# The opening of a fused transformer kernel: first loads, first products and the second tile's contexts in another order

## What is computed

```python
def _L0_xattn_ref(latents, context, ...):
    lat = layernorm(latents, ln_l_w, ln_l_b)
    ctx = layernorm(context, ln_c_w, ln_c_b)
    q = (lat @ Wq)   # 16 heads of 64
    k, v = jnp.split(ctx @ Wkv, 2, axis=-1)
    attn = softmax(clip(einsum('bhnd,bhsd->bhns', q, k) * D ** -0.5, -11, 11))
    return einsum('bhns,bhsd->bhnd', attn, v) @ Wo + bo
...
x = x + _L0_xattn_ref(_layernorm(x), ctx_1024, ...)   # latents are normalised twice
```

## Time and profile before

| | |
|---|---|
| median of 3 runs | 1004.1 us (1000.98 to 1010.59) |
| the profiled execution | 1003.49 us, its span 1001.8 us |
| TensorE busy | 949.6 us, 95% of the span |
| VectorE, ScalarE, GpSimd busy | 613.0, 446.1, 169.3 us |
| mean granted clock of TensorE | 0.981 |

### The profile page before, as it was taken

How to read it: one execution, slowest core, us unless ns; L and a number is a source line. 1 busy time by engine, 2 the same in 40 slices (tenths; PEclk the granted TensorE clock), 3 DMA queues, 4 the chain that set the end, 5 groups by cost and what they waited for, 6 DMA issues and landing times.

```text
span 1001.8 us, 25859 instructions
## 1 busy us (share of the span) xinstructions
PE 949.6 (95%) x10657; PEld 815.0 (81%) x10657; DVE 613.0 (61%) x1448; ACT 446.1 (45%) x892; POOL 169.3 (17%) x357
## 2 busy tenths in 40 slices
PE   5899999999999989999879999997999999999998
PEld 5788888888888777887669999995888888877887
DVE  5655754654532655667798787776787763554242
ACT  3333332433332476654236666652435343673241
POOL 2312112113112213334320000013113000101000
PEclk9999999999999999999979999997999999999999
DMA  9443142131210292000049999952312002000000
GB/s 321 129 106 74 33 106 68 39 85 42 45 37 7 67 381 98 3 12 24 20 129 332 380 357 358 328 129 57 59 36 45 3 2 76 2 2 1 8 14 22
DMA packets 158611, 101.14 MB, mean 101 GB/s; under 512 B 102104, under 2 KB 148128, under 8 KB 157984
## 3 DMA queue, kind: packets, MB, share of 16 engines
q1 hardware_dynamic: 156960, 95.31, 32.0%
q0 software_dynamic: 1536, 4.20, 1.3%
HBM read 82.96 MB, written 16.52 MB: 99 GB/s over the span
## 4 chain that ended last, share of the span: by engine, by line
PE 82%; DVE 9%; ACT 5%; issue 2%; DMA 1%; POOL 0%; SPq 0%; DVEq 0%; ACTq 0%; POOLq 0%
PE ps L642 9%; PE ps L657 8%; PE ps L2367 8%; PE ps L2380 6%; PE ps L2703 6%; PE ps L674 3%; PE ps L1486 3%; PE ps L1195 3%; PE ps L1583 3%; PE ps L596 2%; PE ps L693 2%; PE ps L626 2%; PE ps L1525 2%; PE ps L1120 2%; PE ps L1130 2%
## 5 line engine op out<-in xcount | busy, mean ns | idle before, releaser
L2367 PE MATMUL ps<-moe_xT,ew 128*128 128x128 f32 x736 | 91.3, 278 | 2.2 <-issue 1.2
L2367 PEld LDWEIGHTS ps<-moe_xT,ew 128*128 128x128 f32 x736 | 87.6, 195 | 3.2 <-DVE moe_xT L2453 1.9
L785 ACT ACTIVATE x0pT<-ps 128x512 f32<-128x512 f32 x64 | 38.2, 598 | 111.1 <-PE ps L657 111.1
L1029 POOL TENSOR_SCALAR x0pT<-x0pT 128x512 f32<-128x512 f32 x64 | 40.6, 635 | 188.3 <-ACT x0pT L785 187.2
L2703 PE MATMUL ps<-f,ffw 128*128 128x512 f32 x256 | 60.7, 398 | 0.8 <-issue 0.6
L2703 PEld LDWEIGHTS ps<-f,ffw 128*128 128x128 f32 x256 | 48.9, 192 | 12.0 <-issue 0.9
L642 PE MATMUL ps<-x0wv_hi,x0cT_hi 128*128 128x512 f32 x128 | 53.6, 418 | 4.2 <-DVE x0A_lo L915 4.2
L2380 PE MATMUL ps<-ew_2hi,eh_hi 128*128 128x256 f32 x184 | 55.4, 301 | 1.7 <-DVE eh_lo L2506 1.3
L2316 DVE TENSOR_TENSOR ew_2lo<-ew,ew_2hi 128x1024 fp32r<-128x1024 f32 x46 | 55.9, 1216 | 0.0
L2563 POOL DMA_INDIRECT yg<-moe_out,slot x16 | 16.3, 1017 | 230.9 <-DMA moe_out<-moe_y 163.5
L915 DVE TENSOR_TENSOR x0A_lo<-ps,x0A_hi 128x512 fp32r<-128x512 f32 x64 | 39.8, 683 | 23.4 <-ACT x0A_hi L776 23.3
(11 more groups left out here) (336 smaller groups left out, 2416.6 us busy)
## 6 DMA issues: line engine op xcount, KB each, us to landing
ew<-L_ffn_W_dram SPq DMA_DIRECT2D x46, 1024.0 KB, 7.9
x0cin<-ctx_dram SPq DMA_DIRECT2D x8, 512.0 KB, 4.7
x1cin<-ctx_dram SPq DMA_DIRECT2D x64, 64.0 KB, 2.3
x0cn_rows<-x0cn SPq DMA_DIRECT2D x7, 512.0 KB, 2.8
x0cn_blocks<-x0cn_rows SPq DMA_DIRECT2D x56, 64.0 KB, 2.4
x0att_rows<-x0att SPq DMA_DIRECT2D x14, 256.0 KB, 2.5
x0att_blocks<-x0att_rows SPq DMA_DIRECT2D x56, 64.0 KB, 2.7
moe_out<-moe_y SPq DMA_DIRECT2D x23, 128.0 KB, 4.4
```

The lines of the kernel that those rows point to most:

```text
L785: nc.scalar.activation(g.pT[:, u, :], ps[:, S_BANK[u % 2], :], ACT.Exp, scale=64.0 ** -0.5).then_inc(C0.exp, 1)
L1029: nc.gpsimd.tensor_scalar(g.pT[:, u, :], g.pT[:, u, :], high, low, ALU.min, ALU.max).then_inc(C0.clip, 1)
L2367: last = nc.tensor.matmul(ps[:, n % 3, j * BT:j * BT + BT], ew1[b % NW][:, i, f * P:f * P + P], xT[b % 2][:, i, :], start=(i == 0), stop=( ...
```

## The change

Loads: of the constants only the identity (64 of 297 KB) is loaded at first, the rest behind contexts 1. Opening: TensorE makes 18 products on zeros (pT, set by VectorE) before it waits for any load, then turns key weights, latents and contexts in this order; VectorE normalises the latents ahead of the contexts (norm_first), ScalarE copies K(0) to K(2) and VectorE K(3). Tile 0: turn_context(1), cT(1) and cT_split(1) stand on VectorE and ScalarE behind the work of tile 0, no longer in its middle. SyncE: the 15 loads of later weights are issued behind turn_rows(1).

```diff
-        FILLS = [(("x0", 0), k) for k in ("cT0", "cT1", "K0", "K1", "lat", "K2", "K3", "q0", "q1", "A00", "A01", "A10", "A11", "v0", "v1", "A20", "A21", "A30", "A31")]
+        FILLS = [(("x0", 0), k) for k in ("K0", "K1", "K2", "K3", "lat", "cT0", "cT1", "q0", "q1", "A00", "A01", "A10", "A11", "v0", "v1", "A20", "A21", "A30", "A31")]
...
+            pe.wait_ge(C0.zeros_lat_ones, 1)
+            for _ in range(18):
+                nc.tensor.matmul(ps[:, S_BANK[0], 0:P], g.pT[:, 0, 0:P], g.pT[:, 0, 0:P], start=True, stop=True, skip_group_check=True)
+            pe.wait_ge(ld["const"], 32)
+            for i in range(4):
+                fill_K(i)
+            fill_lat(0)
             fill_cT(0, 0)
             fill_cT(0, 1)
-            fill_K(0)
-            fill_K(1)
-            fill_lat(0)
-            fill_K(2)
-            fill_K(3)
             fill_q(0, 0)
...
+            K(0)
+            K(1)
+            K(2)
+            lat(0)
             cT(0)
-            K(0)
-            lat(0)
-            K(2)
             act.wait_ge(ld["x0v"], 16)
...
                 exp(t, 3)
+                if nxt and t > 0:
+                    cT(t + 1)
                 if nxt:
-                    cT(t + 1)
                     lat(t + 1)
...
+                if t == 0:
+                    cT(1)
...
+            def norm_first():
+                dve.wait_ge(ln_rstd, 1)
+                nc.vector.tensor_scalar(g.lat[:, :], x[:, 0, :], ln_mv[:, 4, 0:1], ln_rs[:, 4:5], ALU.subtract, ALU.mult).then_inc(C0.zeros_lat_ones, 1)
+                dve.sem_inc(dve_go, 1)
+                dve.wait_ge(C0.zeros_lat_ones, 2)
+                nc.vector.bn_stats(g.ln_st[:, 4, :], g.lat[:, :]).then_inc(ln_stats, 1)
+                dve.wait_ge(ln_stats, 2)
+                dve.sem_inc(dve_go, 1)
+                nc.vector.bn_aggr(ln_mv[:, 4, :], g.ln_st[:, 4, :]).then_inc(ln_aggr, 1)
+                for k in range(4):
+                    last = nc.vector.tensor_scalar(g.cn[:, k, :], g.cin[:, 0, k, :], ln_mv[:, k, 0:1], ln_rs[:, k:k + 1], ALU.subtract, ALU.mult)
+                last.then_inc(ln_done, 1)
+                dve.wait_ge(ln_rstd, 2)
+                nc.vector.tensor_scalar(g.lat[:, :], g.lat[:, :], ln_mv[:, 4, 0:1], ln_rs[:, 4:5], ALU.subtract, ALU.mult).then_inc(ln_done, 1)
+
+            nc.vector.memset(g.pT[:, 0, 0:P], 0.0).then_inc(C0.zeros_lat_ones, 1)
             dve.sem_inc(rn_rstd, 2)
             norm(0, 0)
             dve.wait_ge(ld["x"], 16)
             norm(0, 1)
-            norm(0, 2)
+            norm_first()
             dve.wait_ge(ld["const"], 32)
-            norm(0, 3)
+            K(3)
             cT(0)
-            K(1)
-            K(3)
             cT_split(0)
...
-            dve.wait_ge(ld["rest"], 32)
+            dve.wait_ge(ld["rest"], 48)
             for t in range(T):
                 nxt, more = t + 1 < T, t + 2 < T
                 if more:
                     norm(t + 2, 0)
-                if nxt:
+                if nxt and t > 0:
                     turn_context(t + 1)
                 if t > 0:
                     turn_att(t - 1, 0)
                     turn_att(t - 1, 1)
                     v(t, 3)
-                if nxt:
+                if nxt and t > 0:
                     cT(t + 1)
                     cT_split(t + 1)
...
+                    turn_context(1)
+                    cT(1)
                 attend(t, 0)
+                if t == 0:
+                    cT_split(1)
...
-                ln_rstd_pool(pool, 1, 2 * t + 1)
+                ln_rstd_pool(pool, 1, 2 * t + 1, 4 if t == 0 else 0)
...
-            whole(cst[:, :], a["consts"], ld["const"])
+            whole(ident, a["consts"][:, C_IDENT:C_IDENT + P], ld["const"])
             whole(col[:, :], a["cols"], ld["const"])
             whole(X0.wk[:, :, :], weight("L0_xattn_Wkv")[:, :, 0:INNER], ld["x0k"])
             whole(X0.wq[:, :, :], weight("L0_xattn_Wq"), ld["x0q"])
             whole(X0.wv[:, :, :], weight("L0_xattn_Wkv")[:, :, INNER:], ld["x0v"])
             ctx_tile(1, 1)
+            whole(cst[:, P:C_ALL], a["consts"][:, P:C_ALL], ld["rest"])
             whole(X0.wo[:, :, :], weight("L0_xattn_Wo"), ld["x0o"])
             whole(x[:, 2:T, :], x_in[:, 2:T, :], ld["rest"])
...
-            for i, w in enumerate(("wq", "wkv")):
-                whole(w_mla[:, :, 64 * i:64 * i + 64], weight("L0_attn_" + w), ld["mla"])
-            for i, w in enumerate(("wqr", "wqr_swapped", "wkr", "wkr_swapped")):
-                whole(w_mla[:, :, P + P * i:2 * P + P * i], weight("L0_attn_" + w), ld["mla"])
-            whole(w_mlao[:, :, :], weight("L0_attn_wo"), ld["mla"])
-            sp.wait_ge(pool_setup, 4)
-            whole(w_mlac[0:64, 0:P], a["L0_attn_wqc"], ld["mla"])
-            whole(w_mlac[64:P, P:2 * P], a["L0_attn_wkc"], ld["mla"])
-            whole(w_mlac[64:P, 2 * P:2 * P + D], a["L0_attn_wv"], ld["mla"])
-            whole(wg[:, :, 0:E], weight("L0_ffn_Wg"), ld["wg"])
-            for i, w in enumerate(("Wq", "Wk", "Wv", "Wo")):
-                whole(w_sq[0][:, :, i, :], weight("L0_ffn_" + w), ld["sq0"])
             def turn_rows(t):
                 sp.wait_ge(ln_done, 2 * t + 1)
+                if t > 1:
+                    sp.wait_ge(C0.cn_in, 128 * (t - 1))
...
                     turn_rows(t)
+                if t == 1:
+                    for i, w in enumerate(("wq", "wkv")):
+                        whole(w_mla[:, :, 64 * i:64 * i + 64], weight("L0_attn_" + w), ld["mla"])
+                    for i, w in enumerate(("wqr", "wqr_swapped", "wkr", "wkr_swapped")):
+                        whole(w_mla[:, :, P + P * i:2 * P + P * i], weight("L0_attn_" + w), ld["mla"])
+                    whole(w_mlao[:, :, :], weight("L0_attn_wo"), ld["mla"])
+                    sp.wait_ge(pool_setup, 4)
+                    whole(w_mlac[0:64, 0:P], a["L0_attn_wqc"], ld["mla"])
+                    whole(w_mlac[64:P, P:2 * P], a["L0_attn_wkc"], ld["mla"])
+                    whole(w_mlac[64:P, 2 * P:2 * P + D], a["L0_attn_wv"], ld["mla"])
+                    whole(wg[:, :, 0:E], weight("L0_ffn_Wg"), ld["wg"])
+                    for i, w in enumerate(("Wq", "Wk", "Wv", "Wo")):
+                        whole(w_sq[0][:, :, i, :], weight("L0_ffn_" + w), ld["sq0"])
                 if t + 2 < T:
                     sp.wait_ge(ln_done, 2 * t + 2)
                     ctx_tile(t + 2, t % 2)
```

More of the change, by code:

```diff
@@ L321, in ln_statistics, with ln_rstd_pool @@
             last.then_inc(ln_aggr, 1)
-        def ln_rstd_pool(pool, k, idx):
+        def ln_rstd_pool(pool, k, idx, first=0):
+            c = slice(first, first + k)
             pool.wait_ge(ln_aggr, idx + 1)
-            nc.gpsimd.tensor_tensor(ln_ve[:, 0:k], ln_mv[:, 0:k, 1], eps[:, 0:k], ALU.add).then_inc(ln_eps, 1)
+            nc.gpsimd.tensor_tensor(ln_ve[:, c], ln_mv[:, c, 1], eps[:, c], ALU.add).then_inc(ln_eps, 1)
             pool.wait_ge(ln_eps, idx + 1)
-            nc.gpsimd.tensor_tensor(ln_rs[:, 0:k], ln_ve[:, 0:k], neghalf[:, 0:k], ALU.pow).then_inc(ln_rstd, 1)
+            nc.gpsimd.tensor_tensor(ln_rs[:, c], ln_ve[:, c], neghalf[:, c], ALU.pow).then_inc(ln_rstd, 1)
         def ln_apply(dve, srcs, dsts, idx):
@@ L488, in build @@
             cT_lo = sem("c0_cT_lo")
-            ones = sem("c0_ones")
+            zeros_lat_ones = sem("c0_zeros_lat_ones")
             scores = sem("c0_scores")
@@ L546, in build @@
         _more += [(("x1", t), k) for t in range(T) for k in ("q", "k1")]
-        RS = Ring([ps[:, i, :] for i in range(4)], FILLS, ("cT1", "q1", "K1", "K3", "v1", "v3", "v5", "v7", "T1", "rope", "k", "pv", "y", "y2", "router", "rank"),
+        RS = Ring([ps[:, i, :] for i in range(4)], FILLS, ("cT1", "q1", "K3", "v1", "v3", "v5", "v7", "T1", "rope", "k", "pv", "y", "y2", "router", "rank"),
                   SA.fill, SA.by_act, SA.by_dve, _more)
@@ L667, in values @@
                     if t == 0:
-                        pe.wait_ge(C0.ones, 1)
+                        pe.wait_ge(C0.zeros_lat_ones, 3)
                 for par in range(2):
@@ L976, in dve_x0 @@
             A_lower(0, 1)
-            nc.vector.memset(g.v[:, :, :, 64:VW], 1.0).then_inc(C0.ones, 1)
+            nc.vector.memset(g.v[:, :, :, 64:VW], 1.0).then_inc(C0.zeros_lat_ones, 1)
             v(0, 1)
@@ L2962, in _ @@
         def _(pe):
-            pe.wait_ge(ld["const"], 32)
             x0 = pe_x0(pe)
```

## The result

| | before | after |
|---|---|---|
| median | 1002.67 us (20 runs, 999.61 to 1012.33) | 1009.65 us (20 runs, 1005.75 to 1016.18) |
| the profiled execution and its span | 1003.49, 1001.8 us | 1009.19, 1007.5 us |
| TensorE busy | 949.6 us | 957.9 us |
| mean granted clock, profiled execution | 0.981 | 0.976 |

The ratio is 1.0064, with a 95% interval of 1.0043 to 1.0085: the change costs 6 to 7 us. The forecast was 1002.0 with a range to 1008. TensorE is busy 8.3 us longer: 7.1 us are the products on zeros, in a time that was idle, and y(0) alone takes 2.9 us more for the same products.

A forecast was written before the change was run, and what follows sets the result against it. It took TensorE, holding 82% of the span, as the bound. Start -1.7, tile 0 -4.3, new idle before y(0) +2.8 and clock after it +1.7 sum to -1.5 us: from 1003.49 to 1002.0 us, range 996 to 1008.

The forecast's parts named there:

- The bound: Whole kernel: TensorE holds 82% of the span; gains lie only in its idle or slow time in the first stage.
- The start: First 23 us: first value product earlier by 0.8 us with slow transposes, 2.5 with fast ones; 1.7 us taken.
- Tile 0: Middle of tile 0: 2.57 us of idle and 1.7 us of low clock go, together 4.3 us gained.
- rival 4: Tile 0: VectorE's work piles up and v(1,0) waits, giving back up to 2 us, 1004; chance 0.05.
- The place where the gain would stop: At y(0), behind SyncE's chain of issues and landings: it can move forward only by 2.2 us less the rows' delay.
- turn_rows(2) at 49.4: SyncE's queue: behind 15 weight loads taking 8.7 us, this issue comes at 49.4 instead of 51.63, 2.2 us earlier.
- the part on the queue: SyncE's queue before y(0): weights in flight delay the rows 0 to 1.5 us, 0.7 taken; idle becomes 3.0 us.
- The clock after it: Behind the new idle before y(0): lower granted clock costs 1.7 us, as after the 2.57 us gap in tile 0.
- my sum: Whole kernel: start -1.7, tile 0 -4.3, new idle before y(0) +2.8, clock after it +1.7, together -1.5 us.
- The slower one: SyncE's queue: 15 issues take over about 10 us, y(0) idles 6.2 us, clock falls; +2.8, 1006.3; chance 0.12.
- Rival 1: SyncE's queue is quick: y(0) waits 2 us or less, clock stays; -4.5, 999, or -6.8, 996.7; chance 0.28.
- Rival 3: Opening: warm-up has no effect, all 26 transposes take 0.215 us, start gains only 0.8; -0.6, 1002.9; chance 0.13.

The follow-up runs named there:

- e8: The changed kernel once more, unchanged, measured beside e5 and e6; 1008.09 us, ratio 1.0036 to the kernel before.
- e4: The kernel before with only the turn of contexts 1 moved behind the rest of tile 0; 1000.27 us, ratio 0.9965.
- e10: The changed kernel with the eleven small loads back in the opening, only the four w_sq loads behind turn_rows(1); 997.85 us, ratio 0.9916.
- e2: The kernel before with only the 15 loads of later weights moved behind turn_rows(1); 1004.91 us, ratio 0.9996.
- e1: The changed kernel with the 15 loads back behind the load of contexts 2, ahead of turn_rows(1); 997.03 us, ratio 0.9928.
- e9: The changed kernel with the four w_sq loads back in the opening, only the eleven small loads behind turn_rows(1); 1001.92 us, ratio 0.9960.
- e6: The changed kernel with 28 unused products that TensorE makes while it waits for y(0); 1004.96 us, ratio 1.0007 to the kernel before.
- e3: e1 without the 18 products on zeros; 999.33 us, ratio 0.9959 to the kernel before.
- e5: The changed kernel with the 15 loads issued behind both halves of the attention rows of tile 0; 998.95 us, ratio 0.9941.
- e12: e1 with all 297 KB of constants in one first load ahead of the key weights; 1000.96 us, ratio 0.9937 to the kernel before.
- e11: e1 with 28 products on zeros instead of 18; 996.74 us, ratio 0.9912 to the kernel before.

## Why the prediction was wrong

**What held.** The bound, and that there are only two places to gain. The start: forecast 1.7 with ends of 0.8 and 2.5, measured 2.65 in after and 0.25 in e8, the same kernel, by how early the keys land (9.71 and 11.20) and whether they run fast. Both lie outside those ends, so this term held only in its sign. Tile 0: forecast 4.3, measured 4.4, with a clock of 1.00 from 47 to 51, and e4, which has nothing else, puts y(0) 4.5 us earlier beyond its earlier v(0,0). No new wait at v(1,0): I had 57.5 with the turned contexts ready at 53.3, both before the gain of the start, and it is 54.83 and 50.5, so rival 4 did not occur. The place where the gain would stop: y(0), behind a chain of issues and landings. And turn_rows(2) at 49.4 less the start's 1.7, that is 47.7: measured 47.47. Some luck is in that: against the measured start it is 0.7 later than booked, since the block issues of tile 1 took 5.16 us instead of 4.04 and the 15 loads 8.1 instead of 8.7.

**The step that failed** is in the part on the queue: "less what the 2 MB of weights still in flight delay the rows; at 329 GB/s the last megabyte takes 3.1 us and was begun some 3 us earlier, so between 0 and 1.5; I take 0.7". The rows landed 7.2 us after issue instead of 2.8, 4.4 later, and the idle before y(0) was 7.40 us instead of the 3.0 forecast. Two things were wrong in this term. The rate was that of the opening; from 47 to 51 the queues moved 237 GB/s at a DMA share of 0.97. And I left out contexts 3, 512 KB, which stand directly in front of the rows. The four w_sq loads and the contexts are 1.57 MB; at 237 GB/s they take 6.6 us, and the first was issued at 44.84, 2.6 us before the rows: 4.0 us, close to the 4.4 measured. The window of that rate was picked after the result, so the sum is a check and no proof of how the queues share. In other runs it comes out less well or better: e10 and e8 have the same 4.0 and landed 4.7 and 4.8 late, e2 has 1.6 and landed 1.4 late, e1 has 0.3 and landed 0.7 late. The blocks took 5.13 us of issue instead of 4.04, 1.1 more (4.04 again in e8, so this varies), and the attention rows went over their part of the chain 1.2 us faster (60.38 to 70.70, against 59.09 to 70.64), so the end of it came at 75.49.

**The clock after it** was the second mis-sized term, 1.7 booked and 2.9 measured: y(0) took 6.62 us instead of 3.69. I took the loss of the gap of 2.57 us; after a gap of 7.4 the clock is 0.50 until 82 us, nearly all of y(0). e9 is the other side of it: 2.10 us of idle there, and y(0) ran in 3.69. With the wait filled by products (e6) the median is some 3 us lower.

With the measured sizes my sum runs: -2.65 -4.4 +7.2 of additional idle +2.9 = +3.05, and the trace of after has 3.06 at 82.92 and at 118.21. The mechanism was the forecast one, its two prices were too small, and with them the sign came out wrong: y(0)'s start is set by the chain of SyncE (76.17 before, 76.31 after), so the gain of tile 0 is given back there in full, and the idle time then charges the clock on top. The gain of the opening is another thing, since that chain starts with it: turn_rows(1) goes out at 30.73 in after and at 33.13 in e8, v(0,0) starts at 20.02 and 22.42, y(0) at 76.31 and 78.67, with the same idle in front (7.40, 7.36). So in after the chain is 2.8 us longer from the start on than before, and the 2.65 of the opening just hide it.

**The rivals.** The slower one came nearest, +2.8 forecast. Its condition, that the 15 issues take longer than about 10 us, was not met: they took 8.1 us. It was the landing that made its case. I gave it 0.12, since I saw bytes in flight as a small correction to the count of issues. Rival 1 is what e1 shows for the kernel with the loads elsewhere: "with the full 2.5 of the start and no wait at all, -6.8", measured -6.6. Rival 3 is refuted as a rule: after makes 16 key transposes in 1.94 us, and e3, without the zeros, in 3.65. But in four of the ten executions with zeros the keys took 2.93 to 3.52 us, so it describes part of what happens. The rule of the Trainium skill, "TensorE: Matmul & The Clock Gate", Part 4 (PE-mode transpose), that the full clock does not engage for transpose mode, does not agree with these rows.

**The rest of the median.** 3.06 us at y(0) are not the 6.4 of the ratio. I had written that a time over 1008 would mean that something after 80 us moved; only a part of the miss is of that kind. Two things vary between executions. One is the opening: e8 has the late keys and is 4.95 us behind after y(0), for 4.7 of the median. The other is the granted clock further on: after's profiled execution has the two stretches near 362 and 838 us, e8's has not, and such stretches are found in other traces too (0.91 from 780 to 800 us in before, 0.83 from 820 to 840 in e5 and in e12). The mean clock recorded with each execution tells of it: over the runs of before the time falls by 7.1 to 7.5 us for each 0.01 of clock; the medians of the clock are 0.981 for before, 0.978 for e8 and 0.975 for after. From 0.981 to 0.978 is what the place around y(0) makes of the mean: some 10.5 us at half clock are 0.005 of the span, and the four us of before at 0.58, 0.002, are gone. The further 0.003, some 2.3 us, is clock lost elsewhere. Whether the change had a part in that or the session of runs stays open: e8, the same code in another session, does not show it. The interval of e8's ratio, 1.0012 to 1.0060, and that of the first measurement overlap.

Open too is the split of e9's landing, 2.9 us over the 2.8 of before: contexts 3, issued 0.60 us ahead, explain 1.6 of it at 237 GB/s, and the eleven small loads, 1.0 MB over 6.1 us, are less than the queues could move at that rate. Whether their small size slows the queues was not tried.

The best versions are e11, e10 and e1, 0.9912, 0.9916 and 0.9928, which these runs can't put in order: the change with its loads, or in e10 the eleven small ones, issued from about 17 us on, where the opening hides them.

## What to carry to other kernels

A load that nobody waits for soon is not free: ask what stands behind it in its queue, and count two prices, the issues, and the bytes still in flight when the next transfer that somebody waits for is issued, at the rate of that stretch and with every load in between. Where a later product's start is set by a chain of DMAs, moving TensorE's arrival forward gains nothing there and can lose, because after a long wait (7.4 us here) the engine also comes back at a lower clock. And where a step is moved to a later place, ask which buffer it frees: here the turn of contexts 1 became a wait of the queue. Of three edits that touch one chain, test each alone and leave each out: the loads alone cost nothing, and together with the edit that freed their place they cost 9 us or more (e8 against e5, after against e1).
